# The long convolution's taps as one pair of products per tile in the feed-forward stage's last batch, moved between strips by ScalarE

## What is computed

```python
def _L0_ffn_ref(x, ...):              # per token; the butterflies are folded into two matrices
    h = x @ W_exp + b_exp             # 256 -> 1024
    h = gelu(butterfly(h, up) + up_bias)
    y = butterfly(h, down) @ W_con    # 1024 -> 256
    return y + b_con + down_bias

def _L1_attn_a_ref(x, log_dt, log_A_real, A_imag, C_real, C_imag, W, b):
    dt = exp(log_dt)[:, None]
    A = -exp(log_A_real) + 1j * A_imag              # 256 channels x 32 modes
    C = (C_real + 1j * C_imag) * (exp(A * dt) - 1) / A
    vand = exp((A * dt)[:, :, None] * arange(512))
    K = 2 * einsum('dn,dnl->dl', C, vand).real      # the taps: 256 channels x 512
    y = irfft(rfft(x.T, n=1024) * rfft(K, n=1024))[:512]
    return gelu(y.T) @ W.T + b
...
x = x + _L0_ffn_ref(_layernorm(x), ...)
x = x + _L1_attn_a_ref(_layernorm(x), ...)
```

## Time and profile before

| what | value |
|---|---|
| median of 3 runs | 2727.7 us (2725.69 to 2738.58) |
| profiled execution, whole | 2734.7 us |
| its span from first to last instruction | 2732.6 us |
| mean granted TensorE clock | 0.951 |
| TensorE products busy | 2351.7 us (86%) |
| VectorE, ScalarE, GpSimd busy | 58%, 50%, 42% |

### The profile page before, as it was taken

How to read it: one execution, slowest core, us unless ns; L and a number is a source line. 1 busy time by engine, 2 the same in 40 slices (tenths; PEclk the granted TensorE clock), 3 DMA queues, 4 the chain that set the end, 5 groups by cost and what they waited for, 6 DMA issues and landing times. The chain is left out here.

```text
span 2732.6 us, 55617 instructions
## 1 busy us (share of the span) xinstructions
PE 2351.7 (86%) x20720; PEld 1603.5 (59%) x20720; DVE 1596.4 (58%) x4090; ACT 1367.4 (50%) x2100; POOL 1154.2 (42%) x1181
## 2 busy tenths in 40 slices
PE   7957777777999888888888887999789889999979
PEld 4535555555666455455455554666556756666658
DVE  5657778784123567767766762442244446776753
ACT  4522222223232487787787785523111447777653
POOL 4329999981001367645765751000076003323320
PEclk9979999898999899999999999999799989999999
DMA  5464445541001111111111111000000100000001
GB/s 174 131 183 135 139 145 161 151 133 64 0 1 49 40 51 56 49 54 48 59 55 50 56 40 48 1 1 0 2 1 1 37 0 1 1 1 1 1 1 62
DMA packets 158735, 149.04 MB, mean 55 GB/s; under 512 B 21441, under 2 KB 141377, under 8 KB 155393
## 3 DMA queue, kind: packets, MB, share of 16 engines
q1 hardware_dynamic: 138704, 105.51, 13.2%
q0 software_dynamic: 3456, 23.07, 2.5%
q10 hardware_dynamic: 16304, 16.83, 2.1%
HBM read 100.51 MB, written 40.63 MB: 52 GB/s over the span
## 5 line engine op out<-in xcount | busy, mean ns | idle before, releaser
L1612 POOL TENSOR_SCALAR a_dist<-a_dist,a_mq 128x512 f32<-128x512 f32 x512 | 356.9, 717 | 148.5 <-ACT a_mq L1551 148.5
L1655 DVE TENSOR_SCALAR_CACHE_REDUCE a_dist<-a_ring 128x512 f32<-128x512 f32 x512 | 332.5, 686 | 98.1 <-PE a_ring L1300 96.5
L1541 ACT ACTIVATE a_pT<-a_psT 128x1024 f32<-128x1024 f32 x256 | 258.1, 1024 | 120.4 <-PE a_psT L1312 113.6
L1312 PE MATMUL a_psT<-ident,a_dist 128*128 128x128 f32 x2048 | 276.0, 284 | 17.9 <-ACT a_pT L1541 17.8
L1312 PEld LDWEIGHTS a_psT<-ident,a_dist 128*128 128x128 f32 x2048 | 244.8, 147 | 50.2 <-issue 20.3
L1535 ACT ACTIVATE a_dist<-a_dist 128x2048 f32<-128x2048 f32 x128 | 237.0, 1903 | 46.5 <-DVE a_dist L1655 43.5
L1300 PE MATMUL a_ring<-a_stack 102*128 102x512 bf16 x512 | 187.3, 403 | 70.1 <-DVE a_dist L1655 34.8
L1300 PEld LDWEIGHTS a_ring<-a_stack 102*128 102x128 bf16 x512 | 48.4, 98 | 239.1 <-DVE a_dist L1655 165.1
L978 POOL TENSOR_TENSOR c_y<-c_prod 128x1024 f32<-128x1024 f32 x16 | 37.2, 2348 | 334.5 <-DVE c_prod L1011 332.6
L3127 ACT ACTIVATE ds_wtm<-ds_wg,ds_par 128x256 f32<-128x256 f32 x64 | 29.2, 502 | 271.5 <-DVE ds_wg L3257 266.9
L1325 PE MATMUL a_psO<-a_pT,a_va 128*32 128x512 f32 x1024 | 138.9, 619 | 2.3 <-ACT a_pT L1541 2.3
(11 more groups left out here) (416 smaller groups left out, 5461.7 us busy)
## 6 DMA issues: line engine op xcount, KB each, us to landing
a_stack<-a_parts_dram SPq DMA_DIRECT2D x384, 64.0 KB
a_parts_dram<-a_parts SPq DMA_DIRECT2D x32, 384.0 KB, 2.5
bf_w<-in_up_w_dram POOLq DMA_DIRECT2D x10, 1024.0 KB, 6.1
bf_w<-in_down_w_dram POOLq DMA_DIRECT2D x10, 1024.0 KB, 8.0
ds_nbg<-tok_nbk ACTq DMA_DIRECT2D x128, 64.0 KB
feat_v<-di_part SPq DMA_DIRECT2D x16, 256.0 KB, 2.6
tok_nbk<-di_nbk SPq DMA_DIRECT2D x16, 256.0 KB, 3.0
feat_k<-di_part SPq DMA_DIRECT2D x16, 256.0 KB, 3.4
```

Of the source, the lines that this page charges most:

```text
L1312: last = turn(psT[:, u % 2, kb, q * P:(q + 1) * P], dist[:, g % 2, i, q, k * P:(k + 1) * P], core.ident[:])
L1541: a(pT[:, u // 2, u % 2], psT[:, u % 2], ACT.Exp).then_inc(exp_done, 1)
L1612: last = nc.gpsimd.tensor_scalar(d, d, -1.0, mq[:, g % 2, i, q:q + 1], ALU.mult, ALU.add)
L1655: ts(dist[:, gg % 2, i, q, :], ps[:], 1e-12, 3.0e38, ALU.max, ALU.min, accum_out=mq[:, gg % 2, i, q:q + 1]).then_inc(ring_out, 1)
```

## The change

The taps leave `conv_spectra`. In the last batch of the feed-forward stage TensorE makes, behind each of the 8 hidden tiles, the taps of 8 of the 64 tiles: one product with `g_re` and one with `g_im` per tile, now of all 64 columns at once, onto the 32 partitions of strip t % 4. That is 128 products in place of 512. They now land on partitions that the tile number picks, not on those on which they are wanted, so 16 ScalarE instructions (`move_taps`, 4 x 4, each 32 partitions x 256 floats from PSUM to SBUF) move them behind the last gelu. The place they go to is `ck.kT`, now a part of the buffer `ck_f` that is no longer needed then. `psK` (2 banks) is allocated in the feed-forward stage. VectorE's 8 copies and the two waits between TensorE and VectorE go.

```diff
@@ ffn_stage
+        beside.allocate(core, ctx)
...
-            ffn.tensor(pe, lambda b, m: None, bf.back)
+            ffn.tensor(pe, lambda b, m: beside.tensor(nc, pe, b, m), bf.back)
...
             ffn.scalar(act, lambda b: beside.scalar(nc, act, b + 1))
+            beside.move_taps(nc, act)
@@ ConvTaps
+        self.kT = self.f[:, :, 0:D]
...
+        self.psK = core.psum("ck_psK", [P, NMT // TPB, NI * CPT], ctx)
+
+    def tensor(self, nc, pe, b, m):
+
+        per = NMT // FeedForward.NH
+        if b < B - 1:
+            return
+        if m == 0:
+            pe.wait_ge(self.vec, self.TAPS)
+        for t in range(m * per, (m + 1) * per):
+            strip = slice(t % TPB * NJ, (t % TPB + 1) * NJ)
+            for q, g in ((0, self.g_re), (1, self.g_im)):
+                last = nc.tensor.matmul(self.psK[strip, t // TPB, :], g[:, t, :], self.fm[:, q, t, :],
+                                        start=(q == 0), stop=(q == 1))
+        if m == FeedForward.NH - 1:
+            last.then_inc(self.k_ps, 1)
+
+    def move_taps(self, nc, act):
+
+        act.wait_ge(self.k_ps, 1)
+        to = self.kT.rearrange("p k (u q c) -> p q u k c", q=TPB, c=CPT)
+        taps = self.psK[:].rearrange("p u (r k c) -> p r u k c", r=TPB, c=CPT)
+        for q in range(TPB):
+            for r in range(TPB):
+                nc.scalar.activation(to[r * NJ:(r + 1) * NJ, q], taps[q * NJ:(q + 1) * NJ, r],
+                                     ACT.Identity).then_inc(self.kT_done, 1)
@@ conv_spectra
-            pe.wait_ge(ck.vec, ck.TAPS)
-            for t in range(NMT):
-                h, o = t // HT, t % HT * NI
-                for r in range(NI // TPB):
-                    for q, g in ((0, ck.g_re), (1, ck.g_im)):
-                        last = nc.tensor.matmul(psK[strip(r), h, o:o + NI], g[:, t, :],
-                                                ck.fm[:, q, t, r * NI:(r + 1) * NI], start=(q == 0), stop=(q == 1))
-                if t % HT == HT - 1:
-                    last.then_inc(k_ps, 1)
             pe.wait_ge(lc.loaded, 64)
-            pe.wait_ge(kT_done, 2 * TPB)
+            pe.wait_ge(ck.kT_done, TPB * TPB)
...
-            for h in range(2):
-                dve.wait_ge(k_ps, h + 1)
-                dst = kT[:, :, h * D // 2:(h + 1) * D // 2].rearrange("p k (t c) -> p k t c", c=CPT)
-                src = psK[:, h, :].rearrange("p (t k c) -> p k t c", k=TPB, c=CPT)
-                for k in range(TPB):
-                    nc.vector.tensor_copy(dst[:, k], src[:, k]).then_inc(kT_done, 1)
```

More of the change, by code:

```diff
@@ L698, in __init__, with allocate @@
         self.act_n = core.sem("ck_act")
+        self.k_ps = core.sem("ck_k_ps")
+        self.kT_done = core.sem("ck_kT_done")
+        self.kT = self.f[:, :, 0:D]
         self.steps = 0
+    def allocate(self, core, ctx):
+        self.psK = core.psum("ck_psK", [P, NMT // TPB, NI * CPT], ctx)
[20 more added lines that the diff above has]
+                                     ACT.Identity).then_inc(self.kT_done, 1)
     def load(self, sp):
@@ L814, in conv_spectra @@
     with ExitStack() as ctx:
-        HT = NMT // 2
-        kT = core.sbuf("cs_kT", [P, TPB, D], ctx)
-        psK = core.psum("cs_psK", [P, 2, 512], ctx)
+        kT = ck.kT
         psF = core.psum("cs_psF", [P, 2, 512], ctx)
-        k_ps = core.sem("cs_k_ps", ctx)
-        kT_done = core.sem("cs_kT_done", ctx)
         f_ps = core.sem("cs_f_ps", ctx)
@@ L824, in conv_spectra @@
         block = ctx.enter_context(nc.Block())
-        strip = lambda r: slice(r * NJ, (r + 1) * NJ)
         @block.tensor
         def _(pe):
-            pe.wait_ge(ck.vec, ck.TAPS)
-            for t in range(NMT):
-                h, o = t // HT, t % HT * NI
-                for r in range(NI // TPB):
-                    for q, g in ((0, ck.g_re), (1, ck.g_im)):
-                        last = nc.tensor.matmul(psK[strip(r), h, o:o + NI], g[:, t, :],
-                                                ck.fm[:, q, t, r * NI:(r + 1) * NI], start=(q == 0), stop=(q == 1))
-                if t % HT == HT - 1:
-                    last.then_inc(k_ps, 1)
             pe.wait_ge(lc.loaded, 64)
-            pe.wait_ge(kT_done, 2 * TPB)
+            pe.wait_ge(ck.kT_done, TPB * TPB)
             for m in range(2 * NF):
```

## The result

| | median | lowest to highest | runs |
|---|---|---|---|
| before | 2728.52 us | 2725.69 to 2738.58 | 4 |
| after the change | 2704.02 us | 2694.22 to 2705.32 | 4 |

The ratio of the means is 0.9896, with a 95% interval of 0.9861 to 0.993 (the medians alone give 0.991). Executions of a kernel at a lower granted clock than its others, two of ten in e7_three_bursts_scales_late, are left out of the ratios. The forecast was 2702.0 us, the range 2698 to 2713. The profiled execution of the changed kernel took 2705.32 us, its span is 2703.2 us, the mean clock 0.958.

A forecast was written before the change was run, and what follows sets the result against it. TensorE was taken as the path, its taps' products short of instructions. The 28.3 us stretch removed plus 2.4 gained on lc.fwd products minus 5.0 for the moved taps is 25.7 us: 2727.7 becomes 2702.0 us, range 2698 to 2713.

The forecast's parts named there:

- The stretch that goes: From the barrier at 1928.00 to the first lc.fwd product at 1956.28: all 28.3 us leave the path.
- a shortage of instructions: In the old taps stage TensorE lacks instructions: 76 records per us, 27.8 us idle called issue.
- The taps' price on TensorE: Last batch: taps behind hidden tiles add 0.72 us a tile, seven on the path, 5.0 us; bounds 3.0 and 14.8.
- the eighth tile: Last batch: the last hidden tile's taps are hidden in TensorE's 0.78 us wait for the last gelu.
- The visit: Switching TensorE from full-width to 32-partition products and back: 0.11 us entering, 0.14 leaving, 0.25 us per tile.
- The moves: ScalarE's 16 moves behind the last gelu: 8.0 us, hidden with 7 us to spare; bounds 5.3 and 16.4.
- The cover: Time after the last gelu until VectorE's statistics end the block, to hide ScalarE's moves: 15.5 us.
- The second stretch: The lc.fwd products to the end of L874: 14.07 us become 11.65 at full clock, 2.4 us gained.
- The sum: Whole change: 28.3 + 2.4 - 5.0 = 25.7 us gained, giving 2702.0 us.
- strict order: Rival: taps' products on the strips start in program order, 1.55 us a tile, time 2708.4 us; chance 0.2.
- The low clock: Two rivals: clock falls at the lc.fwd stage's start, 2704.4 us, chance 0.08; or throughout last batch, 2744.9 us, chance 0.02.
- The supply of instructions: Last batch: claimed not to bite, 30 records per us needed against 76; if it did, 6.8 us.

The follow-up runs named there:

- e7_three_bursts_scales_late: Changed kernel, taps behind hidden tiles 0, 4 and 7 only (28, 28, 8 tiles), VectorE's row scales after five spectra groups; ratio to the kernel before 0.9897, median 2709.0 us.
- e3_four_times_the_columns: Kernel before, its 512 taps products in the old place widened to 64 columns, plus 16 ScalarE moves; last batch's first hidden product to next stage 77.53 us (before 73.07).
- e8_moves_three_times: Changed kernel with ScalarE's 16 moves made three times, twice to unread places; last batch's first hidden product to next stage 53.49 us (changed kernel 49.30).
- e6_scales_late: Changed kernel with VectorE's row scales behind the first five spectra groups; last batch's first hidden product to next stage 48.48 us (changed kernel 49.30).
- e1_pairs_in_place: Kernel before with the 128 products of 64 columns and 16 moves, but in the old place behind the barrier; ratio to the kernel before 0.9928.
- e5_one_long_burst: Changed kernel, taps of 56 tiles behind the first hidden tile, 8 behind the last; last batch's first hidden product to next stage 48.88 us (changed kernel 49.30).

## Why the prediction was right, point by point

- **The stretch that goes** (28.3 us): right. The barrier is followed by lc.fwd products 1.81 us after L324's end, where the taps came after 1.66, and no TensorE wait of the old stage is left. The reason given, a shortage of instructions, held against columns and clock in e3_four_times_the_columns, and the instruction packets show it.
- **The taps' price on TensorE** (5.0 us): the mechanism was right, the term too small by 0.7. L324 starts 20.40 us after the first hidden product, 14.67 before: 5.73 us. The 32 records were sized well (0.47, measured 0.50), and the eighth tile is hidden in the gelu's wait, of which 0.16 us of 0.78 are left. The visit was mis-sized: 0.25 in the sum, 0.32 in the trace. I had taken it from L1325 and L1300, where the full-width products behind are bf16. Its entering (0.11) and leaving (0.14) were right to 0.02 us. What it lacked are the 0.10 us by which the second record of the first float32 hidden product is late; the bf16 products of L1300 show no such step. Why float32 has it, no run shows.
- **The moves** (hidden, 8.0 us): hidden, and 6.36 us. The short runs of 4 and 16 floats did not make a move longer than the 0.50 us assumed; what they cost by themselves no run shows. The cover was reckoned at 15.5 us, and e8_moves_three_times bears it out to a few tenths.
- **The second stretch** (11.65 us, 2.4 gained): this is the step that failed in part. It took 12.71 us. The clock was at full, as said. What was missing is what stood behind the taps' cover on VectorE: the scales with their table load. I had listed what goes with the taps and not what they had been hiding on another engine. That is 0.82 us (e6_scales_late), and the even pace of the first groups costs 0.24 more than the 0.3 us allowed.
- **The sum**: 25.7 forecast, 23.8 in T. The shortfall of 1.9 is 0.7 for the taps, 1.1 for the second stretch, and 0.1 to 0.2 at the barrier.
- **The rivals**: strict order is refuted by the step of the gelus and the order of starts. One argument against it was a misreading: the earlier trace rows counts every record that touches a microsecond, so neighbours are counted twice. The 211 records of the two microseconds start 9.3 ns apart; the 8.0 ns that were held against the rival's 10 were never measured. Likewise the clock fell at 1930.50 and not at 1930.75. The low clock did not come, neither in the batch nor at the stage's start; its price is seen in e1_pairs_in_place, where TensorE idled over 6 us and the lc.fwd stage took 13.82 us with the scales long done, 1.9 more than at full clock (11.89). The supply of instructions, which I had dismissed at 30 records per us against 76 (rather 70), did not bite in the change, where only three instruction packets came in the whole last batch. But it does where many taps stand in one place: e5_one_long_burst lost 1.5 us to it.

The time missed the forecast by as much as the sum did, 2.0 us (2704.02 against 2702.0) and 1.9. That the two agree is luck: the last batch began anywhere between 1879.5 and 1904.2 us in the traces of these kernels, which share the code ahead of it. T is the test.

## What to carry to other kernels

A run of very small products can be bound by the number of instructions, whatever they compute: look for idle time called issue, double the work per instruction, and see whether the time stands still; then look whether its pieces follow the packets of kind "instruction". Fewer and wider products with a cheap rearrangement on an idle engine are then the larger gain, and a place beside other work comes on top, since it gives the supply time to catch up. When a long stretch is taken off the path, list every engine's queue in it: what it had covered comes out (here a table load and the row scales in front of VectorE's copies).

## What the runs showed of the hardware that I had not expected

- A ceiling of about 70 TensorE instructions (products and weight loads) per us, with 16 and with 64 columns each (1024 product records in 27.0 us in either case) and beside the hidden tiles. It is the pace of the instruction packets: 16384 bytes every 3.7 us, 256 instructions for each. Ahead of it 350 to 420 go freely: 176 product records in one burst, 211 in e1, in e3 and in the kernel before, each with its weight load.
- Where TensorE goes from full-width to 32-partition products and back, it costs 0.32 us, a good half as much as the 32 records (0.50 us) that were visited.
- Records of different strips don't start in the order of the program: eight `g_re` records of four tiles start ahead of the first `g_im`. Four records in a row on one strip do not keep the next strip waiting: 15 ns per record of 64 columns in that order, 14.7 ns with the strip changing at every product, 56 ns on a single strip (1.78 us for 32).
- ScalarE moves 32 partitions x 256 floats from PSUM in 0.40 us each, faster than the 0.50 us of its 128x256 normalizations from SBUF.
